# Local attention of a four-layer model: the product with V in four quadrants of TensorE, the output projection in two column halves, and another order of the programs of all four engines

## The chip, the cores and the metric

The kernel runs on one core of one Trainium2 chip. Times are device microseconds of one execution. The time before is 3204.5 us, the median of three runs (3196.86 to 3204.99).

## The reference, cut to what matters

A model of four layers works on `x` of 128 sequences of 64 tokens and 128 features, all in float32. Each layer is a cross attention and a feed-forward part; the change touches only the last feed-forward part, `L3_ffn`, which is a small transformer of its own and runs two times over (`DEPTH` 2) a local attention and a gated MLP. The attention is this:

```python
h = shift_token(x)                     # half of the features from the token before
q, k, v = jnp.split(h @ wqkv, 3, axis=-1)          # 8 heads of 64
q = l2norm(q) * qs
k = l2norm(k) * ksc
q, k = rotary_xpos(q, k)
sim = einsum('bhwid,bhwjd->bhwij', q * 8.0, k)     # window 64 = a whole sequence, causal
attn = jax.nn.softmax(sim, axis=-1)
o = einsum('bhwij,bhwjd->bhwid', attn, v)
x = x + o @ wo
```

## The kernel before, in words

`x` stays in the core's memory for the whole program, as 64 tiles of 128 tokens (two sequences of 64) by 128 features. Four tiles are a group. A stage is one block in which every engine runs a program written out by hand; the engines meet only through semaphores. The stages of interest are the two calls of `local_attention`, one for each `l`.

In `local_attention` each engine runs `body(g)` for the groups g = -1 to 15, and in it four turns u = 0 to 3, one for each tile of the group. In a turn an engine works on several tiles at different steps of their way, named by how far they are ahead of u. `run_tiles` writes out g = -1, 0 and 15, and loops over the rest. With t for a tile, its way is:

1. PE `transpose_window` (L1944, once per group) and ACT `copy_window` (L2057) make x of a group, tokens along the columns.
2. PE `project_qk` (L1952, L1953) computes q and k of t, 1024 columns in `bank_qk`. It waits for `products` of t-1, that is for DVE to have read the bank.
3. ACT `squares` (L2062); DVE `rotate` (L2169) and `cross`, two halves (L2176), the rotary products; DVE `sum_squares` (L2181, L2184); ACT `roots` (L2067, L2070).
4. POOL `unite` (L2133) adds the products, POOL `normalise_qk` (L2139 to L2146) works out the inverse norm in four small steps and multiplies q and k by it, then signals `unit`.
5. PE `turn_qk` (L1973) transposes q and k when `unit` is there, ACT `copy_qk` (L2081) copies them out, PE `scores` (L1984 the mask, L1992 the 16 products of two heads and two sequences) computes the scores.
6. DVE `maxima` (L2190 the maxima, L2193 the subtraction), ACT `exponentials` (L2085), DVE `sums` (L2201, L2203), POOL `scale_probs` (L2126), PE `turn_probs` (L2003), ACT `copy_pt` (L2090).
7. PE `project_v` (L1963) and ACT `copy_v` (L2075) make the values; PE `weigh_values` (L2017) is the product with V, ACT `copy_ot` (L2095) copies it, PE `project_o` (L2025) projects it, DVE `residual` (L2207) adds it to x.

A matmul in float32 stands in the trace as two records. `weigh_values` has 16 of them, 64 x 64 with 64 columns. In each the row half j (where the weights are read) and the column half (the partitions that the result goes to) are the same, so that they use two of the array's four quadrants:

```python
last = pe.matmul(ps_o[rows, tok], v_rows[rows, at:at + LD], pt[rows, tok], start=True, stop=True)
```

`project_o` has four matmuls on the full array, 128 columns each. The order of a turn, before:

- PE: scores(u+1), project_qk(u+3), project_v(u+3), weigh_values(u), at u = 0 the next group's transpose_window, turn_qk(u+2), project_o(u), turn_probs(u+1).
- ACT: exponentials(u+1), squares(u+3), copy_ot(u), copy_v(u+3), copy_window, copy_qk(u+2), roots(u+3), copy_pt(u+1).
- POOL: scale_probs(u), unite(u+2), normalise_qk(u+2).
- DVE: maxima(u+1), sums(u+1), rotate(u+3), both cross(u+3), sum_squares(u+3), residual(u).

The buffers for products (`rotated_qk`, `crossed_qk`) are double, those for the scores, the probabilities (`pl`, `pt`) and the result (`ot`) single. The weights of this part come by `late_loads`, DMAs that POOL issues in the first cross attention (L749) and that are waited for at its end.

## Time and profile before

| | before |
|---|---|
| median of three runs | 3204.5 us |
| the profiled execution: its own time | 3204.94 us |
| its span, first to last instruction | 3203.2 us |
| mean granted TensorE clock | 0.958 |
| PE matmul busy | 2953.5 us (92%) |
| PE weight load busy | 2076.8 us (65%) |
| DVE busy | 2415.4 us (75%) |
| ACT busy | 1617.7 us (51%) |
| POOL busy | 1146.5 us (36%) |
| first and last start of L2017, 4096 records | 1938.5 and 3044.6 us |

The profile is of one execution. Its page gives each engine's busy time, then the costliest groups of instructions by line; the trace behind it can be asked for the rows of one stretch in order of time, for who waited for whom, and for busy times by stretch. A matmul's end is modelled, and it overlaps with the next one's start, so the time that a group of matmuls takes is best read from its start to the start of what follows. The span on POOL is rough.

### The profile page before, as it was taken

The numbers are of one execution on the slowest core, as the hardware profiler recorded it, in microseconds if no ns is written. First come the engines' busy times: TensorE is split into PE (matmuls) and PEld (weight loads), VectorE is DVE, ScalarE is ACT, GpSimd is POOL, SyncE is SP. The second block draws the span as 40 slices with busy tenths as digits, with TensorE's granted clock in tenths as the row PEclk, the third lists the DMA queues.
The fourth block names the chain that finished last, engine by engine and source line by source line (L and its number), as shares of the span: only waits on it lengthen the run. The fifth ranks groups of instructions, "written<-read, shape, count | busy, mean of one in ns | idle before, by whom it ended". The sixth has DMA issues, their size and how long they took to land. (4 is left out here: it accounts for less than half of the span.)

```text
span 3203.2 us, 101205 instructions
## 1 busy us (share of the span) xinstructions
PE 2953.5 (92%) x37168; PEld 2076.8 (65%) x37200; DVE 2415.4 (75%) x5273; ACT 1617.7 (51%) x2596; POOL 1146.5 (36%) x1289
## 2 busy tenths in 40 slices
PE   6998779997999989998899969999988999999989
PEld 4776657775666657776667746666665566766655
DVE  6887768886777757776678868888876588888756
ACT  3665226663333335554356665666653356666523
POOL 4210322110000011110211208888872278888734
PEclk9999769998999989998999989999999999999999
DMA  3311001110000011210011110000001100000022
GB/s 94 92 40 24 7 11 30 31 30 15 0 0 0 0 24 41 42 40 21 7 32 46 43 33 10 8 10 10 6 4 33 26 8 10 10 9 7 4 81 76
DMA packets 190888, 81.28 MB, mean 25 GB/s; under 512 B 175953, under 2 KB 176528, under 8 KB 190240
## 3 DMA queue, kind: packets, MB, share of 16 engines
q1 hardware_dynamic: 187024, 69.14, 9.3%
q0 software_dynamic: 3728, 10.28, 0.9%
q8 instruction: 91, 1.49, 0.2%
q14 instruction: 45, 0.37, 0.0%
HBM read 37.55 MB, written 8.39 MB: 14 GB/s over the span
## 5 line engine op out<-in xcount | busy, mean ns | idle before, releaser
L596 POOL TENSOR_TENSOR x_norm<-x,mean_all 128x512 f32 (+1 forms) x80 | 83.1, 1039 | 1392.4 <-PE ps_pj L547 783.0
L889 ACT ACTIVATE probs_t<-ps_pt 128x1024 f32<-128x1024 f32 x256 | 262.0, 1023 | 333.9 <-PE ps_pt L1003 332.8
L763 DVE TENSOR_REDUCE row_max<-ps_s 128x16 f32<-128x1024 f32 x256 | 312.5, 1221 | 122.4 <-PE ps_s L992 121.9
L2133 POOL TENSOR_TENSOR kblk<-kblk 128x1024 f32<-128x1024 f32 x128 | 302.1, 2360 | 140.9 <-DVE kblk L2176 140.8
L769 DVE TENSOR_TENSOR probs<-ps_s,row_max 128x1024 f32<-128x1024 f32 x256 | 313.4, 1224 | 16.2
L1025 PEld LDWEIGHTS ps_o<-v,probs_t 128*64 128x64 f32 x8192 | 259.7, 138 | 51.7 <-issue 37.1
L1025 PE MATMUL ps_o<-v,probs_t 128*64 128x18 f32 x8192 | 285.1, 212 | 0.2
L1003 PE MATMUL ps_pt<-ident,probs 128*128 128x128 f32 x2048 | 281.3, 281 | 0.0
L884 ACT ACTIVATE probs<-probs 128x1024 f32<-128x1024 f32 x256 | 268.4, 1049 | 11.8 <-DVE probs L769 11.7
L2146 POOL TENSOR_TENSOR kblk<-kblk,small_d 128x1024 f32<-128x1024 f32 x128 | 243.5, 1902 | 19.0 <-POOL small_d L2143 17.7
L1003 PEld LDWEIGHTS ps_pt<-ident,probs 128*128 128x128 f32 x2048 | 226.8, 143 | 28.8 <-issue 22.6
L1483 ACT ACTIVATE probs<-ps_s 128x512 f32<-128x512 f32 x128 | 76.4, 597 | 226.0 <-PE ps_pt L1430 170.4
L992 PE MATMUL ps_s<-kblk,q_t 32*64 32x256 f32 x4096 | 178.9, 406 | 5.3 <-DVE probs L769 3.2
L2169 DVE TENSOR_TENSOR kblk<-ps_s,rot 128x1024 f32<-128x1024 f32 x128 | 156.7, 1224 | 27.1 <-ACT probs L2062 27.1
L547 PE MATMUL ps_pj<-ident,x_norm 128*128 128x128 f32 x576 | 100.3, 301 | 74.4 <-POOL x_norm L604 48.1
L1439 PEld LDWEIGHTS ps_o<-w,probs 128*128 128x128 f32 x1024 | 133.0, 191 | 49.5 <-issue 25.2
L2176 DVE TENSOR_TENSOR kblk<-ps_s,rot 128x512 f32<-128x512 f32 x256 | 163.5, 679 | 0.0
L2017 PEld LDWEIGHTS ps_o<-big_flat,kblk 64*64 64x64 f32 x4096 | 129.6, 135 | 51.3 <-issue 51.3
L1973 PE MATMUL ps_s<-ident,kblk 128*128 128x128 f32 x1024 | 139.9, 280 | 22.4 <-POOL kblk L2146 19.7
L2201 DVE TENSOR_REDUCE row_max<-big_flat 128x8 f32<-128x512 f32 x128 | 87.8, 686 | 93.9 <-ACT big_flat L2085 93.9
L2181 DVE TENSOR_REDUCE floored<-probs 128x16 f32<-128x1024 f32 x128 | 154.6, 1208 | 0.0
L1952 PE MATMUL ps_s<-w_qkv,q_t 128*128 128x512 f32 x256 | 147.6, 659 | 5.6 <-DVE kblk L2176 4.1
(336 smaller groups left out, 6621.8 us busy)
## 6 DMA issues: line engine op xcount, KB each, us to landing
ci<-in_ctx_t SPq DMA_DIRECT2D x64, 256.0 KB, 3.0
kblk<-k_t SPq DMA_DIRECT2D x688, 16.0 KB
ci<-x SPq DMA_DIRECT2D x64, 128.0 KB
ci<-x SPq DMA_DIRECT2D x128, 63.0 KB
x<-in_x_in SPq DMA_DIRECT2D x4, 1024.0 KB, 8.7
mask<-in_mask_l SPq DMA_DIRECT2D x64, 64.0 KB, 2.5
out<-x SPq DMA_DIRECT2D x16, 256.0 KB, 2.0
out<-x POOLq DMA_DIRECT2D x16, 256.0 KB, 2.3
```

The costliest lines, as they stand in the source:

```text
L763: dve.tensor_reduce(by_group(row_max[u % 2][:, :]), scores_4, AX, ALU.max)\
L769: dve.tensor_tensor(probs[u % 2][:, :, :].rearrange("p (c h) k -> p c h k", c=RG), scores_4, by_group(row_max[u % 2][:, :]).unsqueeze(3).b ...
L884: act.activation(p, p, ACT.Exp, scale=scale).then_inc(exp_ready.sem, 1)
L889: act.activation(probs_t[:, :, :], ps_pt[:, :, :].rearrange("p a (r t) -> p (a r) t", t=P), ACT.Copy).then_inc(pt_ready.sem, 1)
L992: last = pe.matmul(score_banks[b * S:(b + 1) * S, c, :], q_t[par][rows, tok], kblk[par][rows, :, tok], start=plain, stop=True, skip_group_ ...
L1003: last = pe.transpose(ps_pt[:, r // 4, (r % 4) * P:(r % 4 + 1) * P], flat[:, r * P:(r + 1) * P], ident[:, :])
L1025: last = pe.matmul(accumulated[half, 2 * r:2 * r + 2, :], probs_t[:, r, half], v2[par][:, 2 * u + b, r, :, :], start=True, stop=True)
L2133: pool.tensor_tensor(a, a, b_, ALU.add).then_inc(rotated.sem, 1)
L2146: pool.tensor_tensor(a, a, nroot.unsqueeze(2).broadcast_to([P, 2 * LHEADS, LD]), ALU.mult)\
L2169: dve.tensor_tensor(a, by_half(bank_qk), table(0, 0, LD), ALU.mult).then_inc(products.sem, 1)
L2176: dve.tensor_tensor(b_[:, :, :, to:to + HALF], by_half(bank_qk)[:, :, :, of:of + HALF], table(1, to, HALF), ALU.mult).then_inc(products.se ...
L2181: dve.tensor_reduce(floored[:, :, 0], square, AX, ALU.add).then_inc(norms.sem, 1)
```

## The change

- `weigh_values` writes each of its 16 products to a column half that differs with the sequence b (`half = (1 - j if b else j) * S`), so that the four products of a head pair lie in four quadrants, and b = 0 and b = 1 go to two banks. For this `ps_o` and `ps_pj` become one tensor of two banks, and the product and the projection share the second bank; `weigh_values` waits for the residual of the tile before. `copy_ot` (now L2106) reads the two halves.
- `project_o` then has to work sequence by sequence: eight matmuls with 64 columns of weights instead of four with 128, each to 64 partitions, with a second copy of `wo` whose halves are swapped (`w_lo_turned`) for b = 1. It comes by four more DMAs of 128 KB among the `late_loads`.
- The order of a turn is now: PE turn_probs(u), project_v(u+3), weigh_values(u), transpose_window, turn_qk(u+2), project_qk(u+4), project_o(u), scores(u+2). ACT copy_v(u+3), exponentials(u+1), copy_ot(u), copy_window, copy_qk(u+2), roots(u+3), squares(u+4), copy_pt(u+1). POOL unite(u+2), scale_probs(u), normalise_qk(u+2). DVE cross(u+3, 1), maxima(u+1), rotate(u+3), cross(u+3, 0), sum_squares(u+3), sums(u+1), residual(u).

```diff
@@ build_program @@
-        ps_o = ctx.enter_context(nc.psum_tensor("ps_o", [P, 512], F32))
-        ps_pj = ctx.enter_context(nc.psum_tensor("ps_pj", [P, 512], F32))
+        ps_oj = ctx.enter_context(nc.psum_tensor("ps_oj", [P, 2, 512], F32))
+        ps_o, ps_pj = (ps_oj[:, i, :] for i in range(2))
...
+            late_loads += [(w_lo_turned[l][j * S:(j + 1) * S, :, :], w["lo"][l][(1 - j) * S:(2 - j) * S])
+                           for j in range(2)]
@@ local_attention @@
+            weighted = ps_oj[:, :, 2 * P:4 * P]
...
                         wait_tile(pe, ot_copied, g, t - 1)
+                        wait_tile(pe, added, g, t - 1)
...
+                                    half = (1 - j if b else j) * S
-                                    last = pe.matmul(ps_o[rows, tok], v_rows[rows, at:at + LD], pt[rows, tok],
+                                    last = pe.matmul(weighted[half:half + S, b, r * S:(r + 1) * S],
+                                                     v_rows[rows, at:at + LD], pt[rows, tok],
...
-                            last = pe.matmul(ps_pj[:, 0:P], ot[:, r * P:(r + 1) * P], w_lo[l][:, r, :],
-                                             start=r == 0, stop=r == LPAIRS - 1)
+                            for b in range(2):
+                                at = (b * LPAIRS + r) * S
+                                weights = (w_lo, w_lo_turned)[b][l]
+                                last = pe.matmul(ps_pj[b * S:(b + 1) * S, 0:P], ot[:, at:at + S], weights[:, r, :],
+                                                 start=r == 0, stop=r == LPAIRS - 1)
@@ the order on POOL @@
+                            if has_tile(g, u + 2):
+                                unite(g, u + 2)
                             if has_tile(g, u):
                                 scale_probs(g, u)
                             if has_tile(g, u + 2):
-                                unite(g, u + 2)
                                 normalise_qk(g, u + 2)
@@ the order on DVE @@
+                            if has_tile(g, u + 3):
+                                cross(g, u + 3, 1)
                             if has_tile(g, u + 1):
                                 maxima(g, u + 1)
-                                sums(g, u + 1)
                             if has_tile(g, u + 3):
                                 rotate(g, u + 3)
                                 cross(g, u + 3, 0)
-                                cross(g, u + 3, 1)
                                 sum_squares(g, u + 3)
+                            if has_tile(g, u + 1):
+                                sums(g, u + 1)
```

How it stands on the engines. On PE a full turn before, in the part that is written out ahead of the loop, from the scores on:

```order
L1984 MATMUL ps_s<-mask_causal,ident 64x256 x4
L1992 MATMUL ps_s<-big_flat 64x64 x16
L1952 MATMUL ps_s<-w_qkv,q_t 128x512
L1953 MATMUL ps_s<-w_qkv,q_t 128x512
L1963 MATMUL ps_pt<-w_qkv,q_t 64x256 x4
L2017 MATMUL ps_o<-big_flat,kblk 64x64 x16
L1973 MATMUL ps_s<-ident,kblk 128x128 x8
L2025 MATMUL ps_pj<-w_lo,big_flat 128x128 x4
L2003 MATMUL ps_pt<-ident,big_flat 128x128 x4
```

The same place now, from the turning of the probabilities on (L2007 is the old L2003, L1967 the old L1963, L2023 the old L2017, L1977 the old L1973, L1956 and L1957 the old L1952 and L1953, L2035 the old L2025):

```order
L2007 MATMUL ps_pt<-ident,big_flat 128x128 x4
L1967 MATMUL ps_pt<-w_qkv,q_t 64x256 x4
L2023 MATMUL ps_oj<-big_flat,kblk 64x64 x16
L1977 MATMUL ps_s<-ident,kblk 128x128 x8
L1956 MATMUL ps_s<-w_qkv,q_t 128x512
L1957 MATMUL ps_s<-w_qkv,q_t 128x512
L2035 MATMUL ps_oj<-w_lo,big_flat 64x128
L2035 MATMUL ps_oj<-w_lo_turned,big_flat 64x128
```

After the turning of q and k the projection of q and k now comes first, then the output projection (eight matmuls), and only then the scores.

On POOL a turn before:

```order
L2126 TENSOR_TENSOR big_flat<-big_flat,row_max 128x512
L2133 TENSOR_TENSOR kblk<-kblk 128x1024
L2139 TENSOR_TENSOR small_e<-small_d 128x16
L2140 TENSOR_TENSOR small_e<-small_e,small_b 128x16
L2142 TENSOR_SCALAR small_e<-small_e 128x16
L2143 TENSOR_TENSOR small_d<-small_d,small_e 128x16
L2146 TENSOR_TENSOR kblk<-kblk,small_d 128x1024
```

and now:

```order
L2144 TENSOR_TENSOR kblk<-kblk 128x1024
L2137 TENSOR_TENSOR big_flat<-big_flat,row_max 128x512
L2150 TENSOR_TENSOR small_e<-small_d 128x16
L2151 TENSOR_TENSOR small_e<-small_e,small_b 128x16
L2153 TENSOR_SCALAR small_e<-small_e 128x16
L2154 TENSOR_TENSOR small_d<-small_d,small_e 128x16
L2157 TENSOR_TENSOR kblk<-kblk,small_d 128x1024
```

The scaling of the probabilities (L2137) now stands between the sum of the products (L2144) and their normalisation.

On DVE a turn now reads, at the loop's end:

```order
L2188 TENSOR_TENSOR kblk<-ps_s,rot 128x16x32
L2202 TENSOR_REDUCE row_max<-ps_s 128x8
L2205 TENSOR_TENSOR big_flat<-ps_s,row_max 128x2x4x64
L2181 TENSOR_TENSOR kblk<-ps_s,rot 128x1024
L2188 TENSOR_TENSOR kblk<-ps_s,rot 128x16x32
L2193 TENSOR_REDUCE floored<-probs 128x16
L2196 TENSOR_REDUCE small_b<-floored 128x16
L2213 TENSOR_REDUCE row_max<-big_flat 128x8
L2215 RECIPROCAL row_max<-row_max 128x8
L2219 TENSOR_TENSOR x<-x,ps_oj 128x128
```

One half of the cross products stands ahead of the maxima, right behind the residual (L2219) of the turn before, and the sums stand behind the rotation instead of ahead of it.

## Rows read from the trace of the kernel before

**Rows 1.** Busy time by stretch: start and end, length, engines, granted clock, DMA share, GB/s

```profile
1945.00:2375.00 430.00, 423.50 (x5914) 299.20 (x5913) 365.15 (x587) 273.41 (x483) 356.56 (x411) 1.00 0.04 8
...
40.00:80.00 40.00, 37.08 (x600) 27.28 (x600) 30.40 (x50) 24.47 (x35) 13.14 (x21) 0.91 0.16 34
```

**Rows 2.** Timeline (start us, us, ...), PE's V product of tiles 0 and 60, both attentions

```profile
1938.55 1.15 PE L2017 MATMUL ps_o<-big_flat,kblk 64*64 64x64 f32 x32
...
2379.27 1.15 PE L2017 MATMUL ps_o<-big_flat,kblk 64*64 64x64 f32 x32
...
2584.12 1.15 PE L2017 MATMUL ps_o<-big_flat,kblk 64*64 64x64 f32 x32
...
3024.71 1.15 PE L2017 MATMUL ps_o<-big_flat,kblk 64*64 64x64 f32 x32
```

**Rows 3.** Timeline, PE alone, a turn without window transposes, with the window of the turn before

```profile
2232.42 1.15 PE L2017 MATMUL ps_o<-big_flat,kblk 64*64 64x64 f32 x32
2233.50 0.66 PE L1944 MATMUL ps_pt<-ident,ci 128*128 128x128 f32 x4
2234.00 1.04 PE L1973 MATMUL ps_s<-ident,kblk 128*128 128x128 f32 x8
...
2241.35 1.09 PE L1973 MATMUL ps_s<-ident,kblk 128*128 128x128 f32 x8 [0.25 <-POOL kblk L2146]
2242.28 1.06 PE L2025 MATMUL ps_pj<-w_lo,big_flat 128*128 128x128 f32 x8
2243.17 0.60 PE L2003 MATMUL ps_pt<-ident,big_flat 128*128 128x128 f32 x4
2243.70 0.30 PE L1984 MATMUL ps_s<-mask_causal,ident 64*64 64x256 bf16 x4
2243.84 0.63 PE L1992 MATMUL ps_s<-big_flat 64*64 64x64 f32 x32
2244.40 1.13 PE L1952 MATMUL ps_s<-w_qkv,q_t 128*128 128x512 f32 x2
...
2246.31 1.08 PE L1963 MATMUL ps_pt<-w_qkv,q_t 128*64 128x256 f32 x8
2247.33 1.15 PE L2017 MATMUL ps_o<-big_flat,kblk 64*64 64x64 f32 x32
```

**Rows 4.** Timeline, DVE, ACT, POOL and PE on the way from the products on

```profile
2248.71 1.28 DVE L2176 TENSOR_TENSOR kblk<-ps_s,rot 128x512 f32<-128x512 f32 x2
2249.91 1.21 DVE L2181 TENSOR_REDUCE floored<-probs 128x16 f32<-128x1024 f32 x1
2250.17 2.36 POOL L2133 TENSOR_TENSOR kblk<-kblk 128x1024 f32<-128x1024 f32 x1 [0.72 <-DVE kblk L2176]
...
2251.38 0.29 DVE L2207 TENSOR_TENSOR x<-x,ps_pj 128x128 f32 x1
2251.77 0.69 DVE L2190 TENSOR_REDUCE row_max<-ps_s 128x8 f32<-128x512 f32 x1
2252.49 0.21 POOL L2139 TENSOR_TENSOR small_e<-small_d 128x16 f32<-128x16 f32 x1
2252.50 0.69 DVE L2193 TENSOR_TENSOR big_flat<-ps_s,row_max 128x512 f32<-128x512 f32 x1
...
2253.76 1.01 ACT L2062 ACTIVATE probs<-ps_s 128x1024 f32<-128x1024 f32 x1
2253.86 1.90 POOL L2146 TENSOR_TENSOR kblk<-kblk,small_d 128x1024 f32<-128x1024 f32 x1 [0.16 <-POOL small_d L2143]
2253.88 0.69 DVE L2201 TENSOR_REDUCE row_max<-big_flat 128x8 f32<-128x512 f32 x1 [0.69 <-ACT big_flat L2085]
2254.80 1.23 DVE L2169 TENSOR_TENSOR kblk<-ps_s,rot 128x1024 f32<-128x1024 f32 x1
2255.72 1.05 POOL L2126 TENSOR_TENSOR big_flat<-big_flat,row_max 128x512 f32<-128x512 f32 x1
2255.90 1.09 PE L1973 MATMUL ps_s<-ident,kblk 128*128 128x128 f32 x8 [0.20 <-POOL kblk L2146]
```

More of the change, by code:

```diff
@@ L179, in build_program @@
         w_lo = [sb(f"w_lo{l}", [P, LPAIRS, P]) for l in range(DEPTH)]
+        w_lo_turned = [sb(f"w_lo_turned{l}", [P, LPAIRS, P]) for l in range(DEPTH)]
         rot_base = sb("rot_base", [P, 4, LD])
@@ L2030, in body @@
                         for u in range(GT):
-                            now, next_ = has_tile(g, u), has_tile(g, u + 1)
-                            if next_:
-                                scores(g, u + 1)
+                            now = has_tile(g, u)
+                            if now:
+                                turn_probs(g, u)
                             if has_tile(g, u + 3):
-                                project_qk(g, u + 3)
                                 project_v(g, u + 3)
@@ L2042, in body @@
                                 turn_qk(g, u + 2)
+                            if has_tile(g, u + 4):
+                                project_qk(g, u + 4)
                             if now:
                                 project_o(g, u)
-                            if next_:
-                                turn_probs(g, u + 1)
+                            if has_tile(g, u + 2):
+                                scores(g, u + 2)
                     run_tiles(pe, body)
@@ L2094, in copy_ot @@
                         wait_tile(act, y_ready, g, t - 1)
-                        act.activation(ot[:, :], ps_o[:, :], ACT.Copy).then_inc(ot_copied.sem, 1)
+                        act.activation(ot.rearrange("p (b t) -> p b t", b=2), weighted, ACT.Copy)\
+                           .then_inc(ot_copied.sem, 1)
                     def body(g):
                         for u in range(GT):
-                            now, next_ = has_tile(g, u), has_tile(g, u + 1)
-                            if next_:
-                                exponentials(g, u + 1)
-                            if has_tile(g, u + 3):
-                                squares(g, u + 3)
-                            if now:
-                                copy_ot(g, u)
                             if has_tile(g, u + 3):
                                 copy_v(g, u + 3)
+                            if has_tile(g, u + 1):
+                                exponentials(g, u + 1)
+                            if has_tile(g, u):
+                                copy_ot(g, u)
                             if u == 0 and has(g + 1):
@@ L2113, in body @@
                                 roots(g, u + 3)
-                            if next_:
+                            if has_tile(g, u + 4):
+                                squares(g, u + 4)
+                            if has_tile(g, u + 1):
                                 copy_pt(g, u + 1)
@@ L2150, in body @@
                         for u in range(GT):
+                            if has_tile(g, u + 2):
+                                unite(g, u + 2)
                             if has_tile(g, u):
@@ L2217, in body @@
                                 cross(g, u + 3, 0)
-                                cross(g, u + 3, 1)
                                 sum_squares(g, u + 3)
+                            if has_tile(g, u + 1):
+                                sums(g, u + 1)
                             if has_tile(g, u):
```

## The prediction

> **What bounds the kernel now.** The change touches the two local attentions, so I read those. First the busy times by stretch: in 430 us of the first attention PE is busy 423.5, at a granted clock of 1.00, the 2.4 GHz level, DVE 365, POOL 357, ACT 273 [rows 1]. That looks like a stage bound by PE, with DVE and POOL at 85% and 83%.
>
> Then the timeline, to get the turn. From the V product of tile 0 to that of tile 60 it is 440.7 us in the first attention and 440.6 in the second [rows 2], so 7.345 us a turn, over 120 turns in all. PE's own work in a turn follows from start to start [rows 3]: turn_qk 0.93, project_o 0.89, turn_probs 0.53, scores 0.70 (0.14 + 0.56), project_qk 1.91, project_v 1.02 and weigh_values 1.08, in sum 7.06, and 0.50 / 4 = 0.12 for the window: 7.18. That is 0.16 less than the turn. The missing part is a wait: turn_qk at 2241.35 stood idle for 0.25 until POOL's normalisation was done.
>
> So there is a loop of dependences just as long as PE's work. Turn_qk of tile t leads to copy, scores, maxima, exponentials, squares, rotation and cross products of tile t+2, POOL's sum and normalisation, and turn_qk of t+2: two turns, 2241.35 to 2255.90 [rows 3, 4], 14.55 us or 7.28 a turn. PE and this loop hold the time together. An edit that makes only PE shorter gives next to nothing; what counts is what the new order does to such loops.
>
> **The V product.** Now 32 records take 1.08 us in two quadrants, 34 ns each. The 32 records of the scores have the same shape, lie in four quadrants, and take 0.56 [rows 3]. The new product has their pattern, each column half with its two row halves in two banks. I take 0.57, 0.5 less for PE. Should the quadrants not overlap, it stays 1.08; below, that lies in a wait.
>
> **The output projection.** It was 8 records of 128 columns in 0.89 us, and is 16 records with half of the array's columns each. The nearest row is project_v: 8 records, full rows, column halves in turn, 256 columns, 1.02 to the next start and 1.08 to the modelled end [rows 3]. Its column total per half is the same, 1024, but with half as many weight loads. So 1.02 or a little more. The lower bound is today's 0.89, the upper one no overlap of the halves, 16 x 0.111 = 1.78. I take 1.05, with y_ready reaching DVE 1.15 after the start (1.06 modelled end and 0.04 of signal today).
>
> **PE's work in the new turn:** 0.53 + 1.02 + 0.57 + 0.93 + 1.91 + 1.05 + 0.70 + 0.12 = 6.83.
>
> **The new loop.** Take C for the end of the last product of tile t on DVE.
> - POOL: 0.18 to the start of the sum, 2.32 for it (2250.17 to 2252.49). Now scale_probs stands in between: 1.04, by the 1.05 of its row. Then 1.37 for the small steps (2252.49 to 2253.86), 1.90 for the normalisation, 0.14 to PE [rows 4]: 6.95 instead of 5.91. The inverse sums are there in time: behind the products stand sum_squares (1.39 until the residual's start, 2249.99 to 2251.38) and the sums (0.69 and 0.20), 2.3 and 0.2 of signal, against 2.5 for POOL's sum.
> - PE: turn_qk 0.93, then project_qk of t+2, which now stands ahead of the rest, 1.91, then project_o until y_ready, 1.15: 3.99.
> - DVE: residual 0.27 (0.29, the next one starting a little before its end), first cross half 0.60 (half of 2248.71 to 2249.91), maxima 1.39 (0.73 and 0.66), rotation 1.14 (2254.80 to the next products' start, 2255.94), second half 0.68 [rows 4]: 4.08. This is C of tile t+2: its squares are done earlier (project_qk's end, 1.01 for L2062), and so are the scores that the maxima read, 0.2 us ahead of DVE.
>
> Sum: 6.95 + 3.99 + 4.08 = 15.02 for two turns, **7.51 a turn**. Through the scores instead of the residual (project_o 1.05, scores 0.82, maxima 1.42, rotation, second half) the same two turns are 6.95 + 0.93 + 1.91 + 1.87 + 1.42 + 1.14 + 0.68 = 14.90. Both are longer than today's 14.55. The new order takes the sums and half of the cross products out of the loop on DVE, but puts scale_probs on POOL (1.04) and project_qk with the output projection on PE (about 2.9) in, where before PE had copy_qk and the scores at once.
>
> The measured turn before is 0.07 longer than its loop, since every fourth turn has the window and the loop's branch and register instructions. The window (0.50) will now lie in PE's wait, the rest stays: I add 0.05. **7.56 against 7.345, 120 times: +25.8 us.** In that turn PE waits 0.7 at turn_qk. ACT, with 273 of 430 us, keeps its instructions, and copy_ot reads as many elements as before.
>
> **The edges.** Ahead of the 120 turns the scores of tile 0 stand behind one more project_qk and its sums behind a rotation, a good 1 us later for each attention; behind them the last scores come a turn earlier and the last sums wait for no rotation, some 2 us back. Together -1 us. The four added loads, 512 KB, fall in the first cross attention, where POOL was busy 13 of 40 us and the DMA engines 16% [rows 1]: nothing. Without that cover their time by the 34 GB/s of that row is 15 us.
>
> So 3204.9 of the profiled execution (0.4 above the median) + 25.8 - 1 = **3230**.
>
> **The rivals.** About 0.3% (10 us) is what a measurement of this kernel can tell from no change.
>
> *DVE runs ahead, faster.* If the products of a tile are ready 0.8 us before PE comes to project_qk, not 0.35 as by my sum, unit is there when PE arrives, and the POOL leg drops out. What is left is the one-turn loop residual to residual: 4.08 + 0.05 + 1.91 + 1.15 = 7.19, with 0.05 for the loop 7.24; -0.105 x 120 - 1 = -14, so 3191. PE's own 6.83 can't be reached, since the residual stands ahead of the cross products on DVE. For it speaks that DVE has 15% idle; against it that this loop leaves DVE no room to run ahead. It decides at a POOL leg of 6.3 or less. Chance 0.09.
>
> *The two loops cost the same.* The legs come out 0.3 to 0.6 us shorter over two turns, by a shorter y_ready and signals counted twice: 7.27 to 7.43 a turn, 3195 to 3214. For it: the sum for today's loop from the same rows is good only to some 0.1 us. Chance 0.13.
>
> *The column halves don't overlap in project_o.* By the rows, 16 records at 0.111 and a tail of 0.17, y_ready after 1.99: the loop is 15.86, the turn 7.98, +76, 3280. Against it stands project_v, whose eight records of 256 columns would take 1.78 without overlap and take 1.02 [rows 3]. Chance 0.06.
> The Trainium skill bears on this, "TensorE: Matmul & The Clock Gate", "Part 3: Packing small matmuls": weight loads overlap with matmuls in flight only when their row group differs. All 16 records of the new projection use all rows, so by that rule none of the loads would be hidden. With its section on LDWEIGHTS (columns / 1.2 ns) that is an estimate of 16 x 53 ns = 0.85 us more, which is nearly this rival. This trace disagrees as far as project_v goes, where the same holds of the rows.
>
> *PE's clock falls.* PE now waits 0.7 in each turn and is busy 90%. In a stretch with 93% busy the clock was 0.91 [rows 1], so 18% of the time at 1.2 GHz. That adds 0.18 x 3.99 = 0.72 to the loop, 0.36 a turn: +69 with the rest, 3273. Against it: those were a stage's first microseconds, with long gaps. Chance 0.06.
>
> **How the numbers follow.** My forecast has 0.66. Its own range: project_o between 1.06 and 1.30 to y_ready, 0 to 0.15 a turn for the loop's instructions, so 7.47 to 7.73 and 3219 to 3250. Faster by over 0.3% is the first rival, 0.09; within 0.3% the second, 0.13; slower the rest, 0.78. The range that leaves out 2 in 10 reaches down into the second rival, to 3203, and up to 3262; the first, the projection's and most of the clock's stay outside.
>
> **What the new profile would show.** Right: L2023 32 records in 0.57 from start to start; PE busy near 90% of the stage, POOL at 81% and DVE at 83%, each less than before; "L1977 waits for POOL L2157" in nearly every turn, some 0.7 us; scale_probs (L2137) right behind the sum (L2144); DVE waiting for PE's L2035 ahead of each residual; a turn of 7.5 to 7.6. Wrong: turns of 7.3 or less; no wait at L1977; PE waiting at L1956 for DVE instead (the first rival); L2035 taking 1.8 us; a granted clock below 1.00 in the stage.

## The result, and the profile after

| | before | changed |
|---|---|---|
| median, runs of one comparison (6 each) | 3198.71 us (3196.85 to 3204.99) | 3222.36 us (3217.95 to 3226.45) |
| the profiled execution: its own time, its span | 3204.94, 3203.2 | 3220.57, 3218.9 |
| mean granted TensorE clock | 0.958 | 0.961 |
| PE matmul busy | 2953.5 us (92%) | 2916.7 us (91%) |
| DVE, POOL busy | 2415.4, 1146.5 | 2394.2, 1147.8 |

The changed kernel takes 1.0068 times as long as before, 95% interval 1.0058 to 1.0078: slower by 24 us, where 25 were forecast. PE has 37 us less to do and the time goes up.

The extra time lies in the turns of the two attentions. From the start of turn_qk of tile 4 to that of tile 60 (56 turns, tiles counted from 0) a turn takes 7.333 and 7.347 us before, 7.529 and 7.546 now: 0.20 more, 120 times, is 24 us. The two profiled executions differ by 15.6 only. Between turn_qk of tiles 0 and 63 they differ by 9.3 and 13.1, behind it up to the last residual by -0.9 each, so that the attentions carry 20.6 us in this execution and not 24; the other 5 us lie in stages that the change does not touch, which ran that much shorter in this one execution.

Busy time in the same stretch of the first attention as [rows 1], of the changed kernel:

```profile
1945.00:2375.00 430.00, 398.50 (x6215) 260.27 (x6216) 346.13 (x573) 270.34 (x471) 347.53 (x400) 1.00 0.04 8
```

PE went from 423.5 of 430 us to 398.5 (93%), with DVE at 80% and POOL at 81%, at the same clock. No engine is full: the stage waits on a loop. PE's waits in 1960 to 2375, and those of DVE and POOL (engine, what it waited for, us in total, times, longest):

```profile
DVE x L2219 <- PE ps_oj L2035: 65.2, 55, 1.6
POOL kblk L2144 <- DVE kblk L2188: 52.6, 56, 1.3
...
PE ps_s L1977 <- POOL kblk L2157: 26.9, 42, 0.9
```

These three name the loop: residual waits for PE's output projection, POOL's sum for DVE's last product, turn_qk for POOL's normalisation, in 42 of the 55 turns. The same list of before has the last one 21 times, with 5.2 us in all, and no wait of the residual.

PE's turn now, from the timeline. It answers to [rows 3]:

```profile
2226.20 0.30 PE L1988 MATMUL ps_s<-mask_causal,ident 64*64 64x256 bf16 x4
...
2226.90 0.66 PE L2007 MATMUL ps_pt<-ident,big_flat 128*128 128x128 f32 x4
...
2227.49 1.08 PE L1967 MATMUL ps_pt<-w_qkv,q_t 128*64 128x256 f32 x8
...
2228.50 0.69 PE L2023 MATMUL ps_oj<-big_flat,kblk 64*64 64x64 f32 x32
...
2229.82 1.09 PE L1977 MATMUL ps_s<-ident,kblk 128*128 128x128 f32 x8 [0.62 <-POOL kblk L2157]
...
2230.74 1.02 PE L1956 MATMUL ps_s<-w_qkv,q_t 128*128 128x512 f32 x2
...
2231.60 1.02 PE L1957 MATMUL ps_s<-w_qkv,q_t 128*128 128x512 f32 x2
...
2232.55 0.32 PE L2035 MATMUL ps_oj<-w_lo,big_flat 128*64 128x128 f32 x1
...
2233.58 0.30 PE L1988 MATMUL ps_s<-mask_causal,ident 64*64 64x256 bf16 x4
```

From start to start: scores 0.70, turn_probs 0.59, project_v 1.01, turn_qk 0.92, project_qk 1.81, project_o 1.03 (its 16 records come in pairs, 0.108 apart). The V product is followed by a wait here; where the window's transposes follow it, it takes 0.63.

The rest of the loop, DVE and POOL, answers to [rows 4]:

```profile
2226.43 0.29 DVE L2219 TENSOR_TENSOR x<-x,ps_oj 128x128 f32 x1 [1.24 <-PE ps_oj L2035]
2226.63 0.68 DVE L2188 TENSOR_TENSOR kblk<-ps_s,rot 128x512 f32<-128x512 f32 x1
...
2227.23 0.68 DVE L2202 TENSOR_REDUCE row_max<-ps_s 128x8 f32<-128x512 f32 x1
...
2227.95 0.69 DVE L2205 TENSOR_TENSOR big_flat<-ps_s,row_max 128x512 f32<-128x512 f32 x1
...
2228.56 1.21 DVE L2181 TENSOR_TENSOR kblk<-ps_s,rot 128x1024 f32<-128x1024 f32 x1
...
2229.69 0.68 DVE L2188 TENSOR_TENSOR kblk<-ps_s,rot 128x512 f32<-128x512 f32 x1
...
2230.55 2.36 POOL L2144 TENSOR_TENSOR kblk<-kblk 128x1024 f32<-128x1024 f32 x1 [0.86 <-DVE kblk L2188]
...
2232.87 1.04 POOL L2137 TENSOR_TENSOR big_flat<-big_flat,row_max 128x512 f32<-128x512 f32 x1
...
2233.87 0.21 POOL L2150 TENSOR_TENSOR small_e<-small_d 128x16 f32<-128x16 f32 x1
...
2235.24 1.90 POOL L2157 TENSOR_TENSOR kblk<-kblk,small_d 128x1024 f32<-128x1024 f32 x1 [0.16 <-POOL small_d L2154]
```

DVE: residual to the end of the last product, 2226.43 to 2230.37, 3.94. POOL: 0.18 to the start of the sum, 2.32, 1.00 for scale_probs, 1.37 for the small steps, 1.90, and 0.14 to turn_qk: 6.91. PE: turn_qk to residual, 2229.82 to 2233.80, 3.98. Two turns: 14.83, 7.415 a turn.

Four turns take 30.14, though, 0.48 more than twice that. The next turn, with the loop's head and the window, shows where:

```profile
2233.80 0.29 DVE L2219 TENSOR_TENSOR x<-x,ps_oj 128x128 f32 x1 [1.16 <-PE ps_oj L2035]
...
2234.40 0.69 DVE L2188 TENSOR_TENSOR kblk<-ps_s,rot 128x512 f32<-128x512 f32 x1 [0.31 <-issue]
...
2236.70 0.66 PE L1948 MATMUL ps_pt<-ident,ci 128*128 128x128 f32 x4
...
2237.37 1.09 PE L1977 MATMUL ps_s<-ident,kblk 128*128 128x128 f32 x8
2237.55 0.68 DVE L2188 TENSOR_TENSOR kblk<-ps_s,rot 128x512 f32<-128x512 f32 x1
...
2237.76 0.60 ACT L2068 ACTIVATE q_t<-ps_pt 128x512 f32<-128x512 f32 x1
...
2238.58 1.12 PE L1956 MATMUL ps_s<-w_qkv,q_t 128*128 128x512 f32 x2
```

DVE loses 0.31 to "issue" at its loop head (the branch and register instructions between two rounds of its loop), so that its last product ends 4.43 behind the residual and not 3.94. PE starts project_qk 1.21 behind turn_qk and not 0.92: copy_window (L2068) is over only at 2238.36. Which of the two costs the 0.48 is what the last experiments ask. PE has a loop head of its own: once in four turns its turn_probs starts 0.90 behind the scores and not 0.70. These 0.20 go into the wait for POOL as well, and no run takes them away.

### The profile page after: what moved, and what is told of

It reads as the page before. It is cut to its first block and busy times, and to the rows that moved or that the text cites. A ratio compares the mean times of both kernels' runs of the same rounds, so it can differ in the third digit from the quotient of the medians.

```text
span 3218.9 us, 103373 instructions
## 1 busy us (share of the span) xinstructions
PE 2916.7 (91%) x38224; PEld 2002.3 (62%) x38224; DVE 2394.2 (74%) x5273; ACT 1629.0 (51%) x2596; POOL 1147.8 (36%) x1293
## 5 line engine op out<-in xcount | busy, mean ns | idle before, releaser
L2144 POOL TENSOR_TENSOR kblk<-kblk 128x1024 f32<-128x1024 f32 x128 | 301.5, 2356 | 166.1 <-DVE kblk L2188 166.1
L1028 PEld LDWEIGHTS ps_oj<-v,probs_t 128*64 128x64 f32 x8192 | 259.7, 138 | 52.0 <-issue 36.7
L1028 PE MATMUL ps_oj<-v,probs_t 128*64 128x18 f32 x8192 | 285.1, 212 | 0.3
L2188 DVE TENSOR_TENSOR kblk<-ps_s,rot 128x512 f32<-128x512 f32 x256 | 174.9, 683 | 42.1 <-ACT probs L2073 33.8
L1977 PE MATMUL ps_s<-ident,kblk 128*128 128x128 f32 x1024 | 141.9, 282 | 67.0 <-POOL kblk L2157 66.4
L2092 ACT ACTIVATE big_flat<-ps_s 128x1024 f32<-128x1024 f32 x128 | 131.2, 1025 | 81.8 <-PE ps_s L1977 78.9
L2035 PEld LDWEIGHTS ps_oj<-w_lo,big_flat 128*64 128x64 f32 x1024 | 109.6, 138 | 95.4 <-issue 92.0
L1977 PEld LDWEIGHTS ps_s<-ident,kblk 128*128 128x128 f32 x1024 | 111.6, 143 | 88.6 <-issue 73.0
L550 PE MATMUL ps_oj<-ident,x_norm 128*128 128x128 f32 x576 | 100.5, 302 | 72.2 <-POOL x_norm L607 45.9
L2101 ACT ACTIVATE big_flat<-ps_pt 128x512 f32<-128x512 f32 x128 | 76.6, 598 | 174.0 <-PE ps_pt L2007 174.0
L1442 PEld LDWEIGHTS ps_oj<-w,probs 128*128 128x128 f32 x1024 | 133.0, 191 | 49.6 <-issue 25.2
L2073 ACT ACTIVATE probs<-ps_s 128x1024 f32<-128x1024 f32 x128 | 131.5, 1027 | 54.1 <-PE ps_s L1957 54.1
```

Of the source, the lines that this page charges most:

```text
L1028: last = pe.matmul(accumulated[half, 2 * r:2 * r + 2, :], probs_t[:, r, half], v2[par][:, 2 * u + b, r, :, :], start=True, stop=True)
L1442: last = pe.matmul(ps_o[:, u * P:(u + 1) * P], hid[c % SLOTS][:, u * P:(u + 1) * P], w_2[:, c, :], start=c == 0 and u == 0, stop=c == EC - ...
L1977: last = pe.transpose(bank_ts[:, i, r * P:(r + 1) * P], rotated_qk[t % 2][:, i * INNER + r * P:i * INNER + (r + 1) * P], ident[:, :])
L2144: pool.tensor_tensor(a, a, b_, ALU.add).then_inc(rotated.sem, 1)
L2188: dve.tensor_tensor(b_[:, :, :, to:to + HALF], by_half(bank_qk)[:, :, :, of:of + HALF], table(1, to, HALF), ALU.mult).then_inc(products.se ...
```

## The experiments

Each was timed next to the kernel before on the same chip, but not all on one chip, so the ratios compare, not the medians. Turns are the mean over tiles 4 to 60 of each attention.

### The V product and the projection alone, in the old order

```diff
@@ the changed kernel, all four engines @@
-  the new order
+  the order of before
```

> The V product in four quadrants and the output projection in column halves, with the four engines' programs in the order of before. Theory A (two turns are one loop of dependences through POOL, and the V product is not on it): the loop stays 14.55 us, PE's own work falls from 7.18 to about 6.8 a turn, the turn goes from 7.345 to 7.29 to 7.34, 1 to 6 us faster than before. Rival B (the attention is bound by PE's work): the turn falls by 0.35, 42 us faster. Rival C (the change's loss comes from the projection's sixteen half-width records): slower than before by 10 us or more.

Measured: 3215.56 us (3214.19 to 3220.55), ratio 1.0051 [1.0037, 1.0065]; turns of 7.445 and 7.444. Theory A, 1 to 6 us faster, missed, and B too; C holds. Half the V product is saved and the kernel is 15 us slower. The timeline of PE:

```profile
2138.70 1.09 PE L1977 MATMUL ps_s<-ident,kblk 128*128 128x128 f32 x8 [0.61 <-POOL kblk L2157]
2139.72 0.32 PE L2035 MATMUL ps_oj<-w_lo,big_flat 128*64 128x128 f32 x1
...
2140.74 0.66 PE L2007 MATMUL ps_pt<-ident,big_flat 128*128 128x128 f32 x4
2141.33 0.30 PE L1988 MATMUL ps_s<-mask_causal,ident 64*64 64x256 bf16 x4
```

From turn_qk to the scores it takes 2.63, before 2.35 [rows 3]: turn_qk 1.02 where it took 0.93, the projection 1.02 for 0.89, turn_probs 0.59 for 0.53. This stretch lies in the two-turn loop of before (14.55 + 0.28 = 14.83; measured from 2138.70 on 14.98, then 14.82), and the saved V product does not: PE gives it back in waiting for POOL, 41 times, 22.1 us.

### The new order alone

```diff
@@ before, all four engines @@
-  the order of before
+  the new order
```

> The new order of the four programs, with the old V product (two quadrants, one bank) and the old output projection (full width). Theory A: the loop of the new order is 14.83 us in the profile; with the old projection the residual starts 0.15 earlier and project_qk takes its old 1.91, so 14.7 to 14.8, the turn 7.46 to 7.52, 14 to 21 us slower than before; PE's longer V product (1.08) disappears in its wait at turn_qk, which shrinks from 0.6 to 0.1. Rival B (PE's work): PE has the work of before, the same time as before. Rival C (the projection's halves cost the time): the same time as before or faster.

Measured: 3213.55 us (3212.47 to 3214.79), ratio 1.0040 [1.0026, 1.0053]; turns of 7.506 and 7.476. As forecast in the turn; the time is 13 us above before, 14 to 21 were expected. PE waits for POOL here 14 times, 7.3 us, which is the 0.1 a turn of the forecast, but all of it in one turn of four. In another turn PE's own loop head stands open:

```profile
2230.29 0.65 PE L2003 MATMUL ps_pt<-ident,big_flat 128*128 128x128 f32 x4 [0.44 <-issue]
```

So the order alone costs about half of the 24 us, and the two products alone, in the old order, a little more than half.

### POOL in its old order, the rest changed

```diff
-                            if has_tile(g, u + 2):
-                                unite(g, u + 2)
                             if has_tile(g, u):
                                 scale_probs(g, u)
                             if has_tile(g, u + 2):
+                                unite(g, u + 2)
                                 normalise_qk(g, u + 2)
```

> The changed kernel with POOL's order of before: scale_probs(u) first, then unite(u+2) and normalise_qk(u+2). Theory A: on POOL the scaling has to wait for the sums, 2.5 us behind the products, and only then the sum and the normalisation start: the leg from the products to turn_qk becomes 9.25 us instead of 6.91, the loop 17.2, the turn 8.6 to 8.7, 150 to 165 us slower than before, with PE waiting 2 us in each turn at L1977. Rivals B and C: POOL isn't on the path, no difference from the changed kernel (0.7% slower than before).

Measured: 3442.71 us (two runs, 3431.89 and 3453.54), ratio 1.0756 [1.0721, 1.0790]. The direction was forecast, the size not: +242 against 150 to 165. PE also waits otherwise than forecast: 3 us in every second turn instead of 2 in each. The timeline of PE, and the busy times of the stage:

```profile
2195.78 1.97 PE L1977 MATMUL ps_s<-ident,kblk 128*128 128x128 f32 x8 [3.12 <-POOL kblk L2157]
2197.53 1.68 PE L1956 MATMUL ps_s<-w_qkv,q_t 128*128 128x512 f32 x2
...
2199.05 1.02 PE L1957 MATMUL ps_s<-w_qkv,q_t 128*128 128x512 f32 x2
...
2214.90 1.09 PE L1977 MATMUL ps_s<-ident,kblk 128*128 128x128 f32 x8 [2.94 <-POOL kblk L2157]
```

```profile
1945.00:2375.00 430.00, 353.23 (x4890) 226.20 (x4888) 272.40 (x450) 211.08 (x371) 275.31 (x318) 0.89 0.03 7
```

After 3.12 us without work turn_qk takes 1.75 from start to start instead of 0.92, and the first half of project_qk 1.52 instead of 0.86: about twice as long, as at the lower of the two clock levels (1.2 GHz), and the granted clock of the stage is 0.89. The longer wait thus lengthens the legs of the loop behind it as well. It isn't so behind each wait: after the 2.94 at 2214.90 turn_qk takes 0.92, and only the first half of project_qk is slow. Added up from turn_qk to the projection, the slow starts behind the waits make 0.99 of a mean turn of 9.71 in the first attention (from 2000 us on) and 0.52 of 9.17 in the second (from 2752 us on). Without them a turn is 8.72 and 8.65, where 8.6 to 8.7 was said: the clock is what the forecast had left out. Moving scale_probs behind the sum is what makes the rest of the new order usable.

### No scaling on POOL

The kernel leaves out the division of the probabilities by their sums (`scale_probs`); turn_probs waits for the inverse sums alone, and DVE's sums no longer wait for the scaling.

```diff
-                            if has_tile(g, u):
-                                scale_probs(g, u)
```

> The changed kernel without scale_probs on POOL: the probabilities are not divided by their sums; PE's turn_probs waits for the sums instead. Theory A: the POOL leg is 5.9 instead of 6.91, the two-turn loop 13.8 (6.9 a turn), so that the one-turn loop from residual to residual takes over: 1.81 + 1.25 + 3.94 + 0.05 = 7.05, with 0.12 for window and loop 7.17, about 21 us faster than before and 44 faster than the changed kernel. PE then waits for DVE at L1956, not for POOL at L1977. Rival B: 6.83 a turn is PE's work and reached at once, 60 us faster than before, or, if PE's records hold the time as they are now, no difference from the changed kernel.

Measured: 3204.86 us (3199.05 to 3212.44), ratio 1.0015 [1.0004, 1.0026]: by the ratios 17 us less than the changed kernel, where 44 were expected. The plain turns are as forecast, 7.25, 7.25 and 7.12: with 1.0 taken out of POOL's leg PE no longer waits for POOL at all, but at project_qk for DVE (42 times, 12.5 us), the one-turn loop of the residual:

```profile
2106.92 1.12 PE L1955 MATMUL ps_s<-w_qkv,q_t 128*128 128x512 f32 x2 [0.29 <-DVE kblk L2177]
```

The turn with the window takes 8.07: here nothing covers the transposes and the wait for copy_window, which I had left at nothing.

### The column halves alone

```diff
@@ before, project_o @@
-                            last = pe.matmul(ps_pj[:, 0:P], ot[:, r * P:(r + 1) * P], w_lo[l][:, r, :],
-                                             start=r == 0, stop=r == LPAIRS - 1)
+                            for b in range(2):
+                                tok = slice(r * P + b * S, r * P + (b + 1) * S)
+                                last = pe.matmul(ps_pj[b * S:(b + 1) * S, 0:P], ot[:, tok], w_lo[l][:, r, :],
+                                                 start=r == 0, stop=r == LPAIRS - 1)
```

> The kernel before with one thing changed: project_o in two column halves, 16 records instead of 8; V product, order and weights as before, the same result. Theory A2 (in the order of before the loop runs through PE's stretch turn_qk, project_o, turn_probs to the scores; in the kernel with the quadrants alone that stretch was 2.63 us instead of 2.35, because turn_qk ahead of the halves takes 1.02 instead of 0.93, the halves 1.02 instead of 0.89 and turn_probs 0.06 more): the loop becomes 14.83, and PE's own work 7.3 to 7.4 with the window, so the turn 7.45 to 7.50 and the time 13 to 19 us above before. Rival (the quadrants' layout, the shared bank or the two-piece copy_ot costs the time): at most 3 us above before.

Measured: 3224.41 us (3217.27 to 3225.80), ratio 1.0067 [1.0053, 1.0081]; turns of 7.511 and 7.512. The halves alone cost as much as the whole change, 24 us, where 13 to 19 were expected; the rival (at most 3) is out. From the timeline, PE and its weight loads (PEld):

```profile
2232.24 1.09 PE L1973 MATMUL ps_s<-ident,kblk 128*128 128x128 f32 x8
...
2233.26 0.85 PEld L2027 LDWEIGHTS ps_pj<-w_lo,big_flat 128*64 128x64 f32 x16 [0.17 <-issue]
2233.26 1.09 PE L2027 MATMUL ps_pj<-w_lo,big_flat 128*64 128x128 f32 x16
...
2234.28 0.66 PE L2003 MATMUL ps_pt<-ident,big_flat 128*128 128x128 f32 x4
2234.87 0.30 PE L1984 MATMUL ps_s<-mask_causal,ident 64*64 64x256 bf16 x4
```

1.02, 1.02 and 0.59 again. PE's own work in a plain turn is 7.06 + 0.28 = 7.34, and the plain turn measured here is 7.33: with the old V product PE is the bound. The quad_only kernel, which has the V product in four quadrants besides, has turns of 7.445: where PE is the bound the quadrants are worth some 0.07 a turn.

### The halves next to the scores

```diff
@@ the kernel above, the order on PE @@
-                            if now:
-                                project_o(g, u)
                             if next_:
                                 turn_probs(g, u + 1)
+                            if now:
+                                project_o(g, u)
```

> The kernel of halves_only (before, with the projection in column halves) with turn_probs(u+1) ahead of project_o(u) on PE, so that the column halves stand between full-width transposes and the scores, which change the width anyway. Theory S (each change between full and partial width leaves a weight load uncovered, 0.04 behind and 0.09 ahead of the full-width part): turn_qk back to 0.93, turn_probs to 0.53, the halves 1.02: 2.48 from turn_qk to the scores, where halves_only takes 2.63 and before 2.35. A turn 7.51 - 0.15 = 7.36, 18 us below halves_only: 3206 (3204 to 3212). Rival (the halves cost what they cost wherever they stand, by their number of instructions): 2.63, 3221 to 3226.

Measured: 3224.85 us (3222.07 to 3228.52), ratio 1.0076 [1.0062, 1.0090]; turns of 7.532 and 7.533. The timeline bears theory S out, the time (3204 to 3212 was expected) does not:

```profile
2232.75 1.09 PE L1973 MATMUL ps_s<-ident,kblk 128*128 128x128 f32 x8
...
2233.68 0.60 PE L2003 MATMUL ps_pt<-ident,big_flat 128*128 128x128 f32 x4
...
2234.20 1.09 PE L2027 MATMUL ps_pj<-w_lo,big_flat 128*64 128x128 f32 x16
...
2235.23 0.30 PE L1984 MATMUL ps_s<-mask_causal,ident 64*64 64x256 bf16 x4
...
2241.76 0.66 PE L2003 MATMUL ps_pt<-ident,big_flat 128*128 128x128 f32 x4 [0.29 <-ACT q_t L2059]
```

turn_qk 0.93, turn_probs 0.52, the halves 1.03: 2.48, to the hundredth as expected, and PE is busy 422.0 us of 430 instead of 427.4. The time does not move, though: my sum had left out that turn_probs writes the bank from which copy_window reads, and so waits for it in the turn with the window (14 times, 4.1 us). Of four turns (7.55, 7.24, 7.68 and 7.65, against 7.60, 7.33, 7.83 and 7.29 of halves_only) three are shorter, by 0.29 together, and that one is longer by 0.36. So the cost of a change of width is shown; that this order would give it back is not.

### POOL's first small step on ACT

```diff
@@ roots, on ACT @@
+                        wait_tile(act, l_root, g, t, 2)
+                        act.activation(nstep, nroot, ACT.Square).then_inc(l_root.sem, 1)
@@ normalise_qk, on POOL @@
-                        step(pool.tensor_tensor(nstep, nroot, nroot, ALU.mult))
```

> The kernel before with POOL's first small step (the square of the inverse norm's estimate) moved to ACT, right behind the roots: three small steps on POOL instead of four, 0.3 us less between POOL's sum and its normalisation. Theory A: the loop falls from 14.55 to 14.25 and PE's work (7.07 in plain turns, 7.55 with the window) becomes the bound: the turn 7.22 to 7.28, 8 to 14 us faster than before. Rival B (PE's work alone bounds the kernel before): no difference.

> The changed kernel with the same small step moved to ACT. Theory A: its loop falls from 14.83 to 14.53, the turn by 0.15 from 7.54, 18 us faster than the changed kernel: within 0 to 8 us above before. Rival B (PE's work bounds it): no difference from the changed kernel, 0.5 to 0.7% above before.

In the kernel before: 3188.24 us (3186.50 to 3190.98), ratio 0.9960 [0.9946, 0.9973], 12 us faster than before. In the changed kernel: 3209.71 us (3208.19 to 3214.01), ratio 1.0031 [1.0020, 1.0042], by the ratios 12 us faster than the change, where 18 were expected; four turns 29.70 instead of 30.14. Busy times of the first of the two:

```profile
1945.00:2375.00 430.00, 428.60 (x6012) 303.56 (x6012) 370.40 (x597) 290.51 (x552) 348.66 (x356) 1.00 0.04 8
```

PE is busy 428.6 of 430 us, and four turns are 7.14, 7.11, 7.55 and 7.15, close to PE's own 7.06 with 0.50 for the window. Before was held by PE and the loop at once, as the prediction said: with 0.28 off the loop PE alone holds it.

### copy_window ahead of copy_ot

```diff
@@ the changed kernel, the order on ACT @@
-                            if has_tile(g, u):
-                                copy_ot(g, u)
                             if u == 0 and has(g + 1):
                                 copy_window(g + 1)
+                            if has_tile(g, u):
+                                copy_ot(g, u)
```

> The changed kernel with ACT's copy_window ahead of copy_ot instead of behind it. Theory A3 (in one turn of four project_qk waits for the window's copy, start 2238.58 instead of 2238.29, 0.3 us on the loop): 0.3 us less in every fourth turn, 9 us faster than the changed kernel over both attentions, 11 to 15 us above before. Rival (the longer fourth turn comes from register instructions at the loop's head alone): no difference from the changed kernel.

Measured: 3226.63 us (3223.12 to 3227.43), ratio 1.0078 [1.0065, 1.0092]: no gain, as the rival said, where theory A3 had 9 us. The turn with the window:

```profile
2237.71 0.60 ACT L2068 ACTIVATE q_t<-ps_pt 128x512 f32<-128x512 f32 x1
2237.78 0.68 DVE L2188 TENSOR_TENSOR kblk<-ps_s,rot 128x512 f32<-128x512 f32 x1
...
2238.59 1.12 PE L1956 MATMUL ps_s<-w_qkv,q_t 128*128 128x512 f32 x2
```

copy_window now stands 0.8 behind the transposes (2236.92) where it stood 1.1, but project_qk starts at the same time. What it waits for last is the product on DVE that ends at 2238.46 and has DVE's loop head behind it.

### DVE's loop written out, alone and with the edit above

```diff
@@ the order on DVE, in local_attention @@
-                    run_tiles(dve, body)
+                    for g in range(-1, GROUPS):
+                        body(g)
```

> The changed kernel, with DVE's program of both local attentions written out for all groups instead of looped over 14 of them; nothing else is moved. In the changed kernel four turns take 30.14 us. Theory A4 (two chains, each tied to its own tiles): the tiles whose residual stands at DVE's loop head pay 0.49 there (residual to last product 4.43 instead of 3.94, with 0.31 of 'issue' behind L2219), the other tiles pay 0.48 in the turn with the window (project_qk 0.29 later behind turn_qk, and 0.19 of PE's own). Either alone holds the four turns at 30.14, so taking away the loop head alone gives nothing: 3219 to 3226, the head's 0.31 gone from L2188, the window turn as it was. Rival (the loop head is all of the missing 0.28 and the window waits beside it): four turns 29.8, 30 times, 9 us less, 3213.

> The kernel of window_first (copy_window ahead of copy_ot on ACT) with DVE's program of both local attentions written out for all groups. Theory A4: only with both long legs shortened do the four turns get shorter. The window's chain falls to 30.14 - 0.29 = 29.85 (project_qk 0.92 behind turn_qk), the other to 29.65 to 29.85, so 0.3 less, 30 times: 9 us below the changed kernel, 3213 (3210 to 3217). Rival (PE's own work with the window, or the register instructions of the other engines, hold the four turns): no change from window_first, 3223 to 3227.

Alone: 3215.17 us (3210.96 to 3218.27), ratio 1.0051 [1.0037, 1.0064], four turns 29.80. With copy_window first: 3208.77 us (3203.30 to 3212.04), ratio 1.0031 [1.0019, 1.0043], four turns 29.56. Theory A4, of two chains that each hold the turns by themselves, fell: the head alone is worth 0.34 in four turns, as the rival had it (29.8), and both together give twice what A4 said. The 29.56 is 0.10 less than twice the 14.83 added up from the rows of one turn, so that sum is good to no better than this. The timelines of PE, alone and then with the edit:

```profile
2232.83 1.09 PE L1977 MATMUL ps_s<-ident,kblk 128*128 128x128 f32 x8
2233.91 1.12 PE L1956 MATMUL ps_s<-w_qkv,q_t 128*128 128x512 f32 x2
```

```profile
2229.20 1.09 PE L1977 MATMUL ps_s<-ident,kblk 128*128 128x128 f32 x8 [0.15 <-issue]
2230.13 1.02 PE L1956 MATMUL ps_s<-w_qkv,q_t 128*128 128x512 f32 x2
```

project_qk starts 1.08 behind turn_qk without the head, and 0.93, the plain value, when copy_window is early too. My reading is that the two waits end one behind the other: clearing the second (window_first) gives nothing while the head is there, clearing the first gives 0.34, clearing both 0.58.

### All three together

```diff
@@ the changed kernel @@
+  the Square on ACT, copy_window ahead of copy_ot, DVE's loop written out
```

> The changed kernel with the three edits that each shortened it or cleared a wait: POOL's first small step as a Square on ACT (act_square_after), copy_window ahead of copy_ot on ACT, and DVE's program of the local attentions written out for all groups (unroll_window). Theory A5 (the legs add up): four turns 30.14 in the changed kernel, less 0.44 for the shorter POOL leg (29.70 in act_square_after), less 0.58 for head and window (29.56 in unroll_window): 29.12, 7.28 a turn, 30 times 1.02 = 31 us less than the changed kernel: 3192 (3189 to 3198). The order's two-turn loop (14.83 - 0.25 = 14.58, 7.29 a turn) is still longer than PE's own 6.9 and holds it above the 3188 of act_square alone. Rival (with the legs shortened the products are ready before PE comes, and the loop falls to the one-turn loop of the residual, 7.19): 7.20 a turn, 3183 or less, below act_square.

Measured: 3193.98 us (3192.40 to 3202.60), ratio 0.9979 [0.9970, 0.9988]; turns of 7.303 and 7.299, 29.2 for four against 29.12 expected; by the ratios 28 us less than the changed kernel, for 31. The gains add up, and the new order then lies 0.2% under the kernel before, but above it with the one edit on ACT (0.9960). The best version found is the old order with the Square on ACT.

## Why the prediction was right

**The sign and its reason.** Step by step the profile shows what was named: PE less busy than before (93% in the stretch, near 90 was said), POOL at 81%, DVE at 80% (83 was said), turn_qk waiting for POOL's normalisation in 42 of 55 turns, scale_probs right behind the sum, DVE waiting for PE's projection ahead of each residual, a turn of 7.53 to 7.55 where 7.5 to 7.6 was said.

**The sum, against its terms.** POOL's leg 6.95, measured 6.91. DVE's leg 4.08, measured 3.94: the residual gives way to the next product after 0.20, not 0.27, and the pairs overlap a little more than taken. PE's leg 3.99, measured 3.98, but by two errors that cancel: project_qk behind full-width transposes takes 1.81 and not the 1.91 it took behind the scores, and the residual starts 1.25 behind the projection and not 1.15. Together 14.83 for 15.02.

**The term that was mis-sized** is the 0.05 a turn for the loop and the window ("the window will lie in PE's wait, the rest stays"). Four turns have 0.48 over the loop, 0.12 a turn. The window's transposes do fall into PE's wait and use nearly all of it: turn_qk then starts 0.22 behind the end of POOL's normalisation, where it is 0.13 in the plain turns, and the profile shows no wait. What was left out is that DVE's loop head now stands ahead of a product that is in the loop, with the residual it follows, and that project_qk, moved ahead of the projection, reads what copy_window has only just written. By unroll_dve and unroll_window the head is worth 0.34 of four turns and the window behind it 0.24, which is more than the 0.48 by the 0.10 that the rows' loop is too long. So 7.415 + 0.12 = 7.535 was met by 7.51 + 0.05 = 7.56: 0.10 a turn too much in the loop, 0.07 too little around it. The mechanism is shown; that the sum is this close is in part luck. It would have been 8 us too low with the loop right, and 11 us too high with the term around it right.

**The time.** 25 us were forecast and 24 measured. The median came out 8 under 3230 mostly because the forecast started from the profiled execution, 3204.9, and the median of before in this comparison is 3198.7. The two edges were put at -1. In the profiled execution the attentions differ by 20.6, and 120 turns alone make 23.7, so the edges gave -3.1, the two tails -0.9 each of it.

**The V product.** 0.63 where 0.57 was taken, which lies in PE's wait. In the old order the saving doesn't make up for the halves: quad_only is 15 us slower than before. What the old product would cost in the changed kernel no run shows. Its 0.45 more would lie in the wait of 0.62 in a plain turn, but in the turn with the window hardly any wait is left.

**The rivals.** *DVE runs ahead*: its condition, a POOL leg of 6.3 or less, was not reached at 6.91. Without scale_probs the leg is 5.9, and there the one-turn loop shows in plain turns of 7.12 to 7.25, as that rival had it (7.19). *The loops cost the same*: refuted by the interval. *The column halves don't overlap*: 1.03 and not 1.78. The rule of the Trainium skill ("TensorE: Matmul & The Clock Gate", "Part 3: Packing small matmuls"), by which no weight load of these 16 full-row records would be hidden, would by the prediction's estimate have made it 0.85 more; these rows don't agree with it for column halves. The same part also names a second way in which a load is pulled ahead, into the background weight buffer, with which they would agree; no run tells which it is. *PE's clock falls*: it stayed at 1.00 with waits of 0.62; it fell in pool_back, with waits of 2.4 to 3.2.

**What the prediction had as a whole but not in its parts** is the projection's price. It counted 0.13 to 0.16 for project_o. In the old order the halves cost PE 0.28 a turn (2.63 against 2.35), since besides their own 0.13 the full-width work on both sides of them gets longer: 0.09 for turn_qk, 0.06 for turn_probs. In the new order turn_qk is followed by project_qk, also full width, and 0.10 of this comes back there.

## What to carry to other kernels

Where PE and a loop of dependences are equally long, shortening PE's work gives nothing; first find what lies in the loop, here POOL's four small steps, of which one moved to an engine with time to spare was worth 12 us in either order. Count a moved step at the slowest of its turns too, with the loop head or the once-per-group step that now stands ahead of it. And price a matmul in another tile shape by the stretch from the work ahead of it to the work behind, not by its own records.

## What the runs showed of the hardware

**A change of width costs on both sides.** A stretch of full-width transposes takes 0.09 longer from start to start when column halves follow it (1.02 for 0.93), and 0.06 longer when they stand ahead of it (0.59 for 0.53); the weight loads show it as 0.17 of "issue" idle ahead of the first load of the halves. With the halves moved beside the scores, both are gone (halves_late: 0.93 and 0.52); turn_probs then stands ahead of the halves as it stands ahead of the scores in the kernel before, and pays one change there in either. The Trainium skill says in "TensorEngine Tiling (Array Packing)", "Key Properties", that changing the tiling mode drains TensorE; the traces fit that, though they show only the time lost, 0.06 to 0.09 us at a change.

**Column halves of full rows do overlap:** sixteen records of 64 columns of weights, in two column halves by turns, start in pairs 0.108 us apart, as fast as eight records on the full array, at 0.11 each.

**Waits of 2.4 to 3.2 us in every second turn bring matmuls at half speed behind them** (turn_qk 1.75 for 0.92 in pool_back, granted clock 0.89 in the first attention); waits of 0.6 to 0.9 in most turns do not (1.00). The single wait doesn't decide it. In pool_back's first attention all 13 waits of 3.1 us are followed by a slow turn_qk, and 5 of the 13 waits of 2.9; in the second attention 4 of the 11 waits of 3.15 us and more are followed by full speed. At the start of the first attention seven turns in a row have waits of 1.4 to 1.9 us at full speed, and the eighth, of 1.8, is followed by the slow one. So a wait on PE that grows can cost more than its own length.
